# The residual's attention terms: from GpSimd's nine operations a group to TensorE products and one VectorE addition

## The reference, cut to what matters

```
mod = (silu(c) @ wmod).reshape(2, 6, 1, 128);  sa, ca, ga, sb, cb, gb = mod's six parts
ga = sign(ga) * max(|ga|, 0.25)                       (gb the same way)
h  = layernorm(x) * (1 + ca) + sa
q, k, v = linear(h);  qp = h @ Wtq.T + btq            (2 numbers for each token)
attention weights = softmax(q k / sqrt(128), masked by a causal and a distance condition on qp)
output = (weights @ v) @ Wo.T + bo
unit = qp / |qp|
x = x + ga * (h + output + 0.1 * (unit @ Wfq.T + bfq))
h = layernorm(x) * (1 + cb) + sb
x = x + gb * (mixture of 16 experts, 4 chosen for each token, and 2 shared ones)(h)
```

## Time and profile before

| | |
|---|---|
| three timed runs, median | 665.44 us (664.79 to 666.22) |
| the profiled execution | 664.28 us |
| its span, first to last instruction | 662.5 us |
| TensorE busy | 568.8 us (86%) |
| VectorE busy | 512.1 us (77%) |
| ScalarE busy | 362.5 us (55%) |
| GpSimd busy | 362.1 us (55%) |
| mean granted TensorE clock | 0.951 of 2.4 GHz |

### The profile page before, as it was taken

The page is one execution under the profiler, slowest core; times in us unless marked ns, Lnnn a source line. Parts: engine busy times, 40 slices in busy tenths (PEclk is TensorE's granted clock), DMA queues, the critical chain, the costliest instruction groups (busy, mean ns, idle before and its releaser), DMA issues.

```text
span 662.5 us, 10953 instructions
## 1 busy us (share of the span) xinstructions
PE 568.8 (86%) x3524; PEld 342.4 (52%) x3524; DVE 512.1 (77%) x1448; ACT 362.5 (55%) x722; POOL 362.1 (55%) x325
## 2 busy tenths in 40 slices
PE   2846878887877899898989999799988599999995
PEld 1734445565653454354545555465554365656563
DVE  3588899997776688656776675756976999898887
ACT  0623567687642633356775868655455355555552
POOL 4459455844104452869977677733314355555553
PEclk9997679898987799899998999999999999999999
DMA  6501000000004121131112220122100000000000
GB/s 187 159 2 35 1 0 1 1 0 1 1 13 115 69 72 45 63 96 49 63 48 60 69 65 32 51 63 63 49 1 16 2 1 17 2 17 2 17 1 17
DMA packets 21840, 26.01 MB, mean 39 GB/s; under 512 B 2628, under 2 KB 11864, under 8 KB 21784
## 3 DMA queue, kind: packets, MB, share of 16 engines
q1 hardware_dynamic: 21784, 25.33, 13.1%
HBM read 23.09 MB, written 2.23 MB: 38 GB/s over the span
## 4 chain that ended last, share of the span: by engine, by line
PE 42%; DVE 34%; issue 8%; ACT 7%; POOL 6%; SPq 1%; DMA 1%; DVEq 0%; ACTq 0%; POOLq 0%
PE bank L805 7%; PE bank L1053 7%; PE bank L806 7%; PE bank L807 6%; DVE row L1322 4%; PE bank L954 4%; DVE stage L1536 4%; ACT stage L745 4%; DVE pen L1328 3%; DVE row L1333 3%; DVE ysb L1515 2%; PE bank L939 2%; POOL sw L580 2%; PE bank L844 2%; PE bank L914 2%
## 5 line engine op out<-in xcount | busy, mean ns | idle before, releaser
L594 POOL TENSOR_TENSOR gp<-stage,gp 128x512 f16<-128x512 f32 x72 | 83.6, 1161 | 73.6 <-ACT gp L762 73.6
L580 POOL TENSOR_TENSOR sw<-hid,gp 128x512 f32<-128x512 f32 x64 | 81.4, 1271 | 76.9 <-DVE hid L1462 70.4
L1462 DVE SCALAR_TENSOR_TENSOR hid<-stage,bank 128x512 f32<-128x512 f32 x72 | 49.2, 684 | 63.5 <-ACT stage L745 62.1
L745 ACT ACTIVATE stage<-bank 128x512 f32<-128x512 f32 x144 | 84.7, 588 | 22.9 <-PE bank L807 22.6
L762 ACT CAST gp<-stage 128x512 f16<-128x512 f32 x72 | 44.4, 617 | 72.8 <-DVE stage L1536 72.8
L538 POOL TENSOR_TENSOR row<-row,dx 128x512 f32<-128x512 f32 (+3 forms) x48 | 54.6, 1141 | 54.3 <-ACT dx L642 54.0
L699 ACT COPY ptr<-bank 128x512 f32<-128x512 f32 (+2 forms) x80 | 41.5, 518 | 78.2 <-PE bank L939 77.6
L1053 PE MATMUL bank<-stage,wd 128*128 128x512 f32 x144 | 76.7, 615 | 7.2 <-DVE ysb L1467 7.2
L954 PE MATMUL bank<-v,ptr 128*128 128x128 f32 x544 | 77.0, 283 | 3.3 <-DVE x L1308 3.3
L954 PEld LDWEIGHTS bank<-v,ptr 128*128 128x128 f32 x544 | 70.9, 200 | 5.3 <-issue 3.9
L1515 DVE SCALAR_TENSOR_TENSOR ysb<-bank,comb,ysb 128x128 f32<-128x128 f32 x240 | 67.1, 342 | 0.1
(11 more groups left out here) (256 smaller groups left out, 1315.9 us busy)
## 6 DMA issues: line engine op xcount, KB each, us to landing
gp<-shares SPq DMA_DIRECT2D x64, 256.0 KB, 3.1
out_x<-x SPq DMA_DIRECT2D x8, 256.0 KB, 2.3
stage<-in_L_ffn_gate_w SPq DMA_DIRECT2D x1, 576.0 KB, 7.5
stage<-in_L_ffn_up_w SPq DMA_DIRECT2D x1, 576.0 KB, 4.2
stage<-in_L_ffn_gate_w SPq DMA_DIRECT2D x1, 448.0 KB, 6.9
stage<-in_L_ffn_up_w SPq DMA_DIRECT2D x1, 448.0 KB, 3.6
row<-in_L_wmod SPq DMA_DIRECT2D x1, 384.0 KB
stage<-in_L_ffn_sh_gate_w SPq DMA_DIRECT2D x1, 128.0 KB, 5.6
```

The lines of the kernel that those rows point to most:

```text
L580: pool.tensor_tensor(sw[:, s % 2, :], hid[:, s % 2, :], wb[:, n % HELD_WEIGHTS, :], ALU.mult)\
L594: pool.tensor_tensor(gp[:, n % HELD, 1, :], act_g[:, s % 2, :], gp[:, n % HELD, 0, :], ALU.subtract)\
L745: act.activation(sg[:, s % 2, :], gate_bank(s)[:, :], func, scale=half_of / (H_UP * W_UP))\
```

## The change

The base moves from GpSimd to TensorE and VectorE. With hT, diag(ga) and a few bf16 features, a block's base is one fp32 product of hT's 128 columns with the diagonal matrix `diag` (the gated h) plus one product of 21 rows: 3 x 3 bf16 parts of each of the two `unit` columns against those of ga * 0.1 * Wfq, and three rows of ones against the parts of the constants. Both go into the same PSUM range, and VectorE adds a group's 128x512 to x in one operation.

- `unit` becomes two more columns of `quant` (7 instead of 5) and runs through the same three-part split. `fl` grows from 27 to 53 columns, of which 32 to 52 are the new ones; the left features' PSUM range and `flT` have 53 partitions. The distance product uses its first 27 rows as before.
- Once: `gates` also makes `gcol` (ga by feature, on the partitions) and the two diagonal matrices; `value_weights` makes the split columns `tall`; TensorE turns them with two transposes and `turned_terms` copies them out. `spread_terms`, the spreading of ca and sa and three products of `x3b` go.
- The base products of group g are at piece 21 + g, on TensorE and VectorE, for both batches. In the first batch they use banks 5, 6, 7 and 5 again, in the second bank 7 alone, so that each group waits for the addition of the one before. Attention on TensorE begins only when all four groups are added. For the first batch the pieces 21 to 24 are the last before attention; for the second they lie in the mixture's steps 21 to 24.
- GpSimd's nine operations for each of eight groups go. `split`, the roots, `row` and `sw` stay.

```diff
@@ -65,7 +67,7 @@
 VALUES = ({14: (0,), 15: (1,), 16: (2,), 20: (3,)}, {21: (0,), 22: (1,), 23: (2,), 24: (3,)})
-BASE = 18
+BASE = 21
@@ -93,8 +95,6 @@
-BASE_AT = {first + every * n: (g, n) for g, first, every in ((1, 0, 1), (2, 6, 2), (3, 17, 3)) for n in range(5)}
@@ -159,8 +159,9 @@
-    terms = sb("terms", [P, NB, 4, P])
-    share = sb("share", [P, PER, P])
+    gcol = sb("gcol", [P, NB]); gside = sb("gside", [P, 2, NB]); diag = sb("diag", [P, NB, P])
+    tcol = sb("tcol", [P, NB, 3]); trest = sb("trest", [P, NB, 3]); tpart = sb("tpart", [P, 3, NB, 3], BF16)
+    tall = sb("tall", [P, NB, FEAT_LEFT], BF16); trows = sb("trows", [FEAT_LEFT, NB, P], BF16)
@@ -489,45 +499,6 @@
-        def base(b, g, part_of):
-            if g == 0 and part_of == 0:
-                pool.wait_ge(set_dve, 4)
-                pool.wait_ge(unit_ready, b + 1)
-                pool.wait_ge(norm_ready, 2 * BLK * b + BLK)
...
-            if part_of == 4:
-                add_to_x().then_inc(base_ready, 1)
-                pool.wait_ge(base_ready, CH * b + g + 1)
@@ -560,9 +529,8 @@
                 lot = slice(ROOT_AT[n] * PER, (ROOT_AT[n] + 1) * PER)
+                pool.wait_ge(norm_ready, 2 * BLK * b + BLK)
                 norm_root(lot, ROOTS * b + 4 + ROOT_AT[n])
-            if n in BASE_AT:
-                base(b, *BASE_AT[n])
@@ -845,16 +813,15 @@
-                spread_modulation((1, 0), bank[5])
...
                 pe.wait_ge(set_dve, 3)
-                for n in range(3):
-                    last = mm(bank[6][:, n * P:(n + 1) * P], x3b[:, n, :], ident[:, :], start=True, stop=True)
+                for n in range(NB):
+                    last = pe.transpose(bank[6][0:FEAT_LEFT, :].bitcast(BF16)[:, n * P:(n + 1) * P],
+                                        tall[:, n, :], identb[:, :])
@@ -896,6 +864,23 @@
                     mm(bank[2][:, :], selx[:, :], lot, start=True, stop=True).then_inc(spread_made[0], 1)
+            if BASE <= k < BASE + CH:
+                g = k - BASE
+                if b == 0:
+                    pe.wait_ge(set_dve, 4)
+                    if g == CH - 1:
+                        pe.wait_ge(base_added, 1)
+                else:
+                    pe.wait_ge(comb_copied, CH)
+                    if g:
+                        pe.wait_ge(base_added, CH * b + g)
+                for j, i in enumerate(range(g * PER, (g + 1) * PER)):
+                    dst = base_bank(b, g)[:, j * P:(j + 1) * P]
+                    mm(dst, hT[:, i * P:(i + 1) * P], diag[:, b, :], start=True, stop=False)
+                    last = mm(dst, flT[FEAT_UNIT:FEAT_LEFT, i * P:(i + 1) * P], trows[FEAT_UNIT:FEAT_LEFT, b, :],
+                              start=False, stop=True)
+                last.then_inc(base_made, 1)
@@ -903,6 +888,7 @@
                 pe.wait_ge(v_ready, CH * (b + 1))
+                pe.wait_ge(base_added, CH * (b + 1))
@@ -1139,6 +1125,18 @@
                                           op0=ALU.add, op1=ALU.mult))
+            gate = md[:, 2, :]
+            step(dve.tensor_scalar(gside[:, 0, :], gate, 0.0, 2.0, ALU.is_ge, ALU.mult))
+            step(dve.scalar_tensor_tensor(out=gside[:, 1, :], in0=gate, scalar=-1.0, in1=gate,
+                                          op0=ALU.mult, op1=ALU.max))
+            settle()
+            step(dve.tensor_scalar(gside[:, 1, :], gside[:, 1, :], NEAR, None, ALU.max))
+            settle()
+            step(dve.scalar_tensor_tensor(out=gcol[:, :], in0=gside[:, 0, :], scalar=-1.0, in1=gside[:, 1, :],
+                                          op0=ALU.add, op1=ALU.mult))
+            settle()
+            for b in range(NB):
+                step(dve.tensor_scalar(diag[:, b, :], ident[:, :], gcol[:, b:b + 1], None, ALU.mult))
@@ -1152,25 +1150,28 @@
             settle()
-            for n in range(3):
-                step(dve.tensor_scalar(x3b[:, n, :], ones[:, :], x3[:, n:n + 1], None, ALU.mult))
+            for b in range(NB):
+                step(dve.tensor_scalar(tcol[:, b, :], x3[:, :], gcol[:, b:b + 1], None, ALU.mult))
+            settle()
+            step(dve.tensor_copy(tpart[:, 0, :, :], tcol[:, :, :])); settle()
+            step(dve.tensor_tensor(trest[:, :, :], tcol[:, :, :], tpart[:, 0, :, :], ALU.subtract)); settle()
+            step(dve.tensor_copy(tpart[:, 1, :, :], trest[:, :, :])); settle()
+            step(dve.tensor_tensor(trest[:, :, :], trest[:, :, :], tpart[:, 1, :, :], ALU.subtract)); settle()
+            step(dve.tensor_copy(tpart[:, 2, :, :], trest[:, :, :])); settle()
+            for b in range(NB):
+                for n in range(2):
+                    o = FEAT_UNIT + 9 * n
+                    step(dve.tensor_copy(tall[:, b, o:o + 9].rearrange("p (s t) -> p s t", s=3),
+                                         tpart[:, :, b, n].unsqueeze(1).broadcast_to([P, 3, 3])))
+                step(dve.tensor_copy(tall[:, b, FEAT_LEFT - 3:FEAT_LEFT], tpart[:, :, b, 2]))
...
-        def spread_terms():
+        def turned_terms():
             dve.wait_ge(set_pe, 5)
-            step(dve.tensor_copy(x3b[:, :, :], bank[6][:, 0:3 * P])); settle()
-            for b in range(NB):
-                gate = gbc[:, b, 0:1, :]
-                ca, sa = (bank[5][:, (2 * b + n) * P:(2 * b + n + 1) * P] for n in range(2))
-                step(dve.scalar_tensor_tensor(out=terms[:, b, 3, :], in0=ca, scalar=1.0, in1=gate[:, 0, :],
-                                              op0=ALU.add, op1=ALU.mult))
-                step(dve.tensor_tensor(terms[:, b, 2, :], sa, x3b[:, 2, :], ALU.add))
-                step(dve.tensor_tensor(terms[:, b, 0:2, :], x3b[:, 0:2, :], gate.broadcast_to([P, 2, P]), ALU.mult))
-            settle()
-            for b in range(NB):
-                step(dve.tensor_tensor(terms[:, b, 2, :], terms[:, b, 2, :], gbc[:, b, 0, :], ALU.mult))
+            step(dve.tensor_copy(trows[:, :, :].rearrange("p b d -> p (b d)"),
+                                 bank[6][0:FEAT_LEFT, :].bitcast(BF16)[:, 0:NB * P]))
@@ -1229,11 +1230,8 @@
                 dve.wait_ge(root_ready, ROOTS * b + 2)
-                if b:
-                    dve.wait_ge(base_ready, CH * b)
-                dve.tensor_tensor(unit[:, :, :], qp[:, :, :], runit[:, :].unsqueeze(2).broadcast_to([P, BLK, 2]),
-                                  ALU.mult).then_inc(unit_ready, 1)
+                step(dve.tensor_tensor(quant[:, :, 5:7], qp[:, :, :],
+                                       runit[:, :].unsqueeze(2).broadcast_to([P, BLK, 2]), ALU.mult))
@@ -1260,13 +1258,17 @@
                                          by_part(a).unsqueeze(2).broadcast_to([P, BLK, 3, 3])))
+                for n in range(2):
+                    o = FEAT_UNIT + 9 * n
+                    step(dve.tensor_copy(fl[:, :, o:o + 9].rearrange("p i (s t) -> p i s t", t=3),
+                                         by_part(5 + n).unsqueeze(3).broadcast_to([P, BLK, 3, 3])))
...
             if k == POSITIONS + 4 and b == 0:
-                spread_terms()
+                turned_terms()
@@ -1287,6 +1289,13 @@
                        .then_inc(spread_ready[0], 1)
+            if BASE <= k < BASE + CH:
+                g = k - BASE
+                dve.wait_ge(base_made, CH * b + g + 1)
+                own = x[:, b * BLK + g * PER:b * BLK + (g + 1) * PER, :]
+                dve.tensor_tensor(own, own, base_bank(b, g)[:, :].rearrange("p (k d) -> p k d", d=P), ALU.add)\
+                   .then_inc(base_added, 1)
@@ -1303,7 +1312,7 @@
                 dve.wait_ge(turned_used, NCH * b + CHUNKS_BEFORE[i + 1])
-                dve.wait_ge(base_ready, CH * b + i // PER + 1)
+                dve.wait_ge(base_added, CH * b + i // PER + 1)
```

More of the change, by code:

```diff
@@ L44 @@
 FEAT = 27
+FEAT_UNIT = 32
+FEAT_LEFT = FEAT_UNIT + 21
 TINY = 1e-30
@@ L322, in pooled, with base_bank @@
             return b * NCH + m - POOL_FROM + 1
+        def base_bank(b, g):
+            return bank[(5, 6, 7, 5)[g] if b == 0 else 7]
         def gate_bank(s):
@@ L440, in _ @@
             chain.step(pool.memset(fl[:, :, :], 0.0))
+            chain.step(pool.memset(tall[:, :, :], 0.0))
             chain.step(pool.memset(minus_half[:, :], -0.5))
@@ L468, in _ @@
             chain.step(pool.memset(fl[:, :, 21:24], HUGE))
+            chain.step(pool.memset(fl[:, :, FEAT_LEFT - 3:FEAT_LEFT], 1.0))
             chain.settle()
@@ L491, in split @@
                 pool.tensor_tensor(dst[:, 1, lot, :], w, dst[:, 0, lot, :], ALU.subtract).then_inc(stage_used, 1)
-            def base(b, g, part_of):
-                if g == 0 and part_of == 0:
-                    pool.wait_ge(set_dve, 4)
-                    pool.wait_ge(unit_ready, b + 1)
-                    pool.wait_ge(norm_ready, 2 * BLK * b + BLK)
-                own = x[:, b * BLK + g * PER:b * BLK + (g + 1) * PER, :]
-                def add_to_x():
-                    return pool.tensor_tensor(own, own, share[:, :, :], ALU.add)
-                def spread(n):
```

(24 more changed lines are left out.)

26 lines of the change are left out of this document (13 added, 13 removed).

## The result

The changed kernel took 676.17 us (median of 4 runs, 673.47 to 679.00); the kernel before, run beside it, 665.83 (4 runs). The ratio is 1.0151, with a 95% interval of 1.0124 to 1.0178: about 10 us slower. The forecast was 670.8 with a range up to 676.0: the sign was right, the size half of what it is. The profiled execution of the changed kernel is its fastest, 673.47 us with a span of 671.4; that of before has 664.28 and 662.5.

What follows compares the result with a forecast made beforehand. No one engine was taken to bound the kernel: VectorE in the first attention, TensorE beside the mixture. Terms +3.5 - 3.4 + 0.3 + 7.7 - 2.7 = +5.4 us on 664.28 gave 669.7, 670.8 in timed runs; range 665 to 676.

Steps and rivals of the forecast that it cites:

- Part 1: First batch up to the first base product: shorter VectorE chain with fewer stalls behind GpSimd, base ready 6.0 us earlier.
- Part 2: Base products on TensorE: +9.5 us in the first batch, a third at the low clock, and +7.7 in the second.
- Part 3: First batch's attention: VectorE operations no longer stretched beside the removed GpSimd operations, -3.4 us.
- up to the second base: Second batch, two more `fl` copies in the chain before L844: +0.3 us.
- Part 4: 293 to 326 us: `sw` and `row` come in time on GpSimd, freeing holes in TensorE's row, -2.7 us.
- behind it: After 330 us: TensorE's row has next to no holes, so nothing follows from GpSimd's rest.
- Rival (c): All of the first base at the low clock, or a switch behind fp32 costs 0.15 us or more: 674; chance 0.13.
- The switch: Base products on TensorE: each change between full-height and 21-row matmuls costs 0.10 us, 32 changes a batch.
- Rival (e): Base products: every weight load is exposed at about 0.1 us, 9.3 us a batch, 11 in the first: 673.9; chance 0.04.
- Rival (a): Base products: small product's weight load hidden behind the fp32 pass, switches free: 662.4 to 664, faster; chance 0.12.
- rival (d): First batch: VectorE's stalls are not GpSimd's and stay, so +9.8 us in all, 675.2; chance 0.04.

Runs made afterwards that it cites:

- experiment 2: The changed kernel with the small products padded by zeros from 21 rows to full height, order kept: 665.93 us, ratio 1.0005 to the kernel before.
- experiment 1: The changed kernel with each group's four fp32 products first and its four 21-row products behind them: 666.05 us, ratio 1.001 to the kernel before.
- 3: The changed kernel with the second batch's base products and additions left out: 669.87 us, ratio 1.0081 to the kernel before.
- experiment 4: The changed kernel with 20 unread fp32 products filling TensorE's waits ahead of the first base: 674.1 us, ratio 1.0128 to the kernel before.
- 9: The changed kernel with full-height small products, grouped behind the fp32 ones, at the same places: 661.5 us, ratio 0.9938 to the kernel before.
- experiment 7: experiment 2 plus nine GpSimd additions a group on an unread tile, in the second batch only: 665.19 us, ratio 0.9984 to the kernel before.
- Experiment 6: experiment 2 plus nine GpSimd additions a group on an unread tile, in the first batch only: 672.63 us, ratio 1.0107 to the kernel before.
- experiment 8: The changed kernel with full-height small products, fp32 ones grouped first, the first batch's diag products moved into earlier TensorE waits: 654.71 us, ratio 0.9828.
- experiment 10: experiment 8 with 21-row small products again, grouped behind the diag ones: 659.37 us, ratio 0.9897 to the kernel before.

## Why the prediction was right in its sign and wrong in its size

The terms by the prediction's own steps (profiled executions, us):

| step | predicted | measured |
|---|---|---|
| Part 1, base may start | -6.0 | -7.3 |
| Part 2, first base | +9.5 | +15.1 |
| Part 3, first attention | -3.4 | -3.2 |
| up to the second base | +0.3 | -2.1 |
| Part 2, second base | +7.7 | +8.8 |
| Part 4, 293 to 326 | -2.7 | -3.6 |
| behind it | 0 | +1.5 |
| sum | +5.4 | +9.2 |

**The step that failed is the size of the first base's term in Part 2.** "The base products themselves keep it busy. I take a third of them at the low level: 9.5 us." All sixteen pairs ran at 1.2 GHz, 16 x 0.94 = 15.0 us (15.1 by the table). Against the forecast that is +5.6, more than the whole miss of 3.8. Of it 3.4 is the clock: the prediction's own price for a base wholly at the low level was 12.9. The other 2.2 is the pair, 0.94 us there instead of the 0.80 that the 12.9 stands for. Rival (c) named the case of the clock and gave it 0.13 with 674. It was the likelier one by the rows: the clock stood at 0.50 at just that place, and in the kernel before it stayed there for 8 us more although TensorE had no gap:

```profile
70.00:78.00 8.00, 8.00 (x28) 3.55 (x29) 7.46 (x21) 4.45 (x13) 3.67 (x4) 0.50 0.01 3
```

The prediction's words that the base products "themselves keep it busy" take for granted what this row speaks against. The experiments show what the clock did with each stream, in one trace each. Full-height products had the full clock again some 6 us into the base (experiment 2, at about 69.2), grouped 21-row products 9 us into it (experiment 1, at about 73.6), alternating 21-row ones never (the changed kernel, 3 and 4). Where these began at the full clock (4), they lost it 3.1 us later with no gap ahead of them. Why is open.

**The switch was found, and mis-sized.** The prediction read 0.10 us for each change between full height and 27 rows off; the pair was to take 0.48 and took 0.575. The small product is as foretold (0.155). The missing 0.10 is in the fp32 product behind it, 0.42 instead of 0.32; at full height 0.06 of it is still there (0.28 instead of 0.22). Experiments 1, 2 and 9 take it apart. A group of four pairs at the full clock, in us:

| | alternating | grouped |
|---|---|---|
| 21 rows | 2.20 | 1.32 |
| full height | 1.28 | 1.12 |

So height costs 0.92 for four pairs (0.23 a pair, there and back), the alternation of fp32 and bf16 products at equal height 0.04 a pair, and nothing is left when both are gone. Rival (e), every load exposed, falls with the last cell: eight fp32 passes and four bf16 matmuls, each with its own weight load, take their columns. The Trainium skill (TensorE: Matmul & The Clock Gate, "The mechanism") says that a load overlaps running matmuls only where the row group differs; the sentence ahead of it also lets a load into a background weight buffer go ahead. The measurement decides against the first here, since the fastest stream, 1.12 us, is the one in which no row group differs. Rival (a) falls with the first.

The two misses in the second batch nearly cancelled, which is luck: the products took 8.8 us instead of 7.7, all of it on the path (attention's first matmul is 11.35 us later, the V product ahead of the base 2.5), and Part 4 brought 3.6 instead of 2.7. The 2.1 us ahead of the second base are not what the forecast had there. The trace of before has a low-clock stretch at 275.9 to 279.5 that the one after hasn't; by the eight matmuls ahead of the V product it is worth 1.6 us (276.30 to 280.04 against 280.38 to 282.54). All ten experiments have such a stretch in that stage. The changed kernel's profiled execution is its fastest, and no record shows whether its slower ones have it.

**Part 1 and Part 3 were right, and for the reason given.** VectorE's chain ended at 50.95 (50.4 foretold), with two stalls of 2.2 and 2.3 us behind `split(1)`. The size of Part 1 holds to some 3 us only: experiments 1 and 7 have VectorE's chain over at 51.2 as well, but their first base begins at 64.6 and 64.7, not at 61.6, with TensorE's clock at 0.50 for some us between 52 and 62. VectorE's timeline of the changed kernel:

```profile
45.32 2.17 DVE L1241 TENSOR_SCALAR quant<-quant,thr 128x16 f32<-128x16 f32 x1
...
47.78 2.32 DVE L1244 TENSOR_TENSOR rest<-quant,parts 128x112 f32<-128x112 f32 x1
...
50.39 0.27 DVE L1246 TENSOR_TENSOR rest<-rest,parts 128x112 f32<-128x112 f32 x1
```

The same subtraction takes 2.32 us at 47.78 and 0.27 at 50.39. Experiment 6 puts the load back alone, with nobody waiting for its results, and pays 6.7 us (5.4 by the spans); rival (d) falls.

**Part 4 had about the right size and a reason that is confirmed in part.** The holes of TensorE at 292 to 330 are gone (38.00 busy of 38); by the mixture's down product at 330.33 (338.67 after) that is 3.0 us. But experiment 7 loads GpSimd nearly as before, and only 0.9 us of them come back. What the kernel before has beyond it is that VectorE waits for the results, and that its operations are longer (1.22 us against 1.06). The other 2.1 us lie there by elimination; that isn't shown.

**Why even the two bases together don't explain the loss.** Left out one at a time they are worth 14 and 5 to 6 us, some 20 in all; the change is 10 slower. The other 10 are what it wins elsewhere: by GpSimd's rest, 6.7 of them by experiment 6, and by VectorE's shorter list (`spread_terms` gone), which no run parts from it. This sum takes it that the pieces add up. The idea of the change was good for some 10 us, and its two streams of products cost twice that.

## What to carry to other kernels

Before small-K products are put between full ones, group them, or pad the short operand to full height with zeros: the columns are paid anyway, and the switch is worth more than the whole product. Where work is added behind a wait, price it at the clock that the trace grants at that place, and look first for an earlier place where its inputs are already there. And a chain of waits that runs through a full engine names a suspect: load that engine alone before a gain is booked on it (here that gave 0.9 us of 3.0).

## What was not expected of the hardware

- An fp32 full-height product and a 21-row bf16 one of 128 columns each, alternating, take 0.575 us a pair where the columns are 0.275: 0.10 more ahead of the small product, 0.10 in it and 0.10 in the fp32 product behind it. With 128 rows the pair takes 0.335 (0.06 more, in the fp32 product). At 1.2 GHz the pair is 0.94 against 0.64.
- TensorE's granted clock fell to 0.50 at 69.4 us in experiment 4, after 11 us without a gap, and stayed there for some 17 us. In the changed kernel it stayed low for 24 us (about 60.4 to 84.2), with TensorE at 14.72 of 15 from 62 to 77. The short base products aren't needed for a long stretch of this kind: experiment 8 has none, and its clock is low from about 60.4 to 74.0, with TensorE at 2.00 of 2.00 in each window of two us from 66 to 74. The Trainium skill (TensorE: Matmul & The Clock Gate, "HAM oscillation — how this bites in real kernels") puts such falls down to gaps in TensorE's work; the fall of experiment 4 had none that the trace shows.
- Matmuls on different rows of the array can run at the same time: in experiment 10 four 21-row products (partitions 32 to 52) start at 58.08, 0.01 us behind a 27-row one of 512 columns (partitions 0 to 26, 58.07), and both take what they take alone (0.39 and 0.37 us).
- A VectorE operation with two SBUF inputs beside a GpSimd one took up to 2.85 us instead of 0.74 (experiment 6, at 102.80, beside `split`'s L507; 1.47 at 107.87 beside the stand-ins), though neither waits for the other. The Trainium skill (SBUF — State Buffer, "Who interferes with whom") says that such a VectorE operation contends with a GpSimd one that reads SBUF, and the trace agrees.
